# Moving the folding of W_v behind the placing of the scores in an attention and FFN kernel

## The reference, cut to what matters

```python
x: (64, 750, 1); W_tok: (512, 128); Wq, Wk, Wv, Wo: (512, 512); 16 heads of 32
patches = x[:, starts[:, None] + arange(128)]            # 10 positions, stride 64
h = patches @ W_tok.T + b                                # (64, 10, 512)
y = layernorm(h)
q, k, v = y @ Wq.T, y @ Wk.T, y @ Wv.T                   # by head; rope on q and k
scores = causal(q @ k.T / sqrt(32))
heavy = key with the largest sum of softmax(scores) over the queries
probs = softmax(scores where key is heavy or |i - j| <= 1)
h = h + (probs @ v) @ Wo.T
y = layernorm(h)
gate, up = split(y @ w_gate_up.T)                        # 2 x 2048
h = h + (silu(gate) * up) @ w_down.T
```

## Time and profile before

| | |
|---|---|
| median of 3 runs | 288.92 us (288.78 to 289.41) |
| the profiled execution | 288.86 us |
| its span, first to last instruction | 286.9 us |
| TensorE busy | 274.6 us, 96% |
| VectorE busy | 160.8 us, 56% |
| ScalarE busy | 80.3 us, 28% |
| POOL busy | 54.7 us, 19% |

### The profile page before, as it was taken

One profiled execution on the slowest core, in us unless ns is written; L12 is line 12 of the kernel. 1 busy time (PEld: TensorE's weight loads), 2 busy tenths in 40 slices (PEclk: granted clock), 3 DMA queues, 4 the chain that ended last, 5 costly groups with the idle time before them and its releaser, 6 DMA issues.

```text
span 286.9 us, 4588 instructions
## 1 busy us (share of the span) xinstructions
PE 274.6 (96%) x1781; PEld 215.9 (75%) x1781; DVE 160.8 (56%) x309; ACT 80.3 (28%) x151; POOL 54.7 (19%) x44
## 2 busy tenths in 40 slices
PE   7979999998899999999999999999999999999994
PEld 6455477664586877776876666799999999999993
DVE  2582987779669998696904435463333334333323
ACT  2211123431321001423011103263434444343320
POOL 0123000001006150003600000133222222332210
PEclk9999999999999999999999999999999999999999
DMA  7992130000002524353412033286334433330003
GB/s 226 425 404 82 43 112 0 5 2 0 1 2 110 163 102 177 116 193 130 144 77 73 37 112 111 110 271 243 110 111 146 148 142 110 110 110 0 0 0 110
DMA packets 6816, 32.76 MB, mean 114 GB/s; under 512 B 977, under 2 KB 977, under 8 KB 6289
## 3 DMA queue, kind: packets, MB, share of 16 engines
q1 hardware_dynamic: 6512, 32.15, 32.0%
q10 hardware_dynamic: 288, 0.39, 0.4%
HBM read 31.23 MB, written 1.31 MB: 113 GB/s over the span
## 4 chain that ended last, share of the span: by engine, by line
PE 91%; DVE 4%; ACT 1%; issue 1%; POOL 0%; DVEq 0%
PE ps L210 35%; PE ps L1076 20%; PE ps L1086 10%; PE ps L1013 6%; PE ps L951 4%; PE ps L1005 4%; PE ps L966 3%; PE ps L929 2%; PE ps L956 2%; PE ps L882 2%; PE ps L1018 1%; DVE prod L238 1%; PE ps L993 1%; PE ps L935 1%; DVE stats L553 1%
## 5 line engine op out<-in xcount | busy, mean ns | idle before, releaser
L210 PE MATMUL ps<-xT,wgu 128*128 128x384 f32 x384 | 70.9, 340 | 0.1
L210 PEld LDWEIGHTS ps<-xT,wgu 128*128 128x128 f32 x384 | 68.1, 188 | 2.5 <-DVE xT L584 0.9
L1076 PE MATMUL ps<-whole,stage 128*128 128x256 f32 (+1 forms) x288 | 58.3, 357 | 1.4 <-ACT whole L369 1.4
L1076 PEld LDWEIGHTS ps<-whole,stage 128*128 128x128 f32 x288 | 49.6, 190 | 12.2 <-issue 4.8
L789 DVE TENSOR_TENSOR gu<-silu,ps 128x256 f32<-128x256 f32 (+1 forms) x32 | 15.5, 484 | 67.6 <-PE ps L210 44.7
L303 POOL TENSOR_TENSOR wd<-stage,wd 128x512 fp32r<-128x512 f32 x16 | 26.9, 1681 | 78.6 <-ACT wd L369 78.6
L210 PE MATMUL ps<-wd,hT 128*128 128x512 f32 x144 | 35.6, 393 | 0.0
L474 ACT ACTIVATE silu<-ps 128x256 f32<-128x256 f32 (+1 forms) x32 | 14.0, 438 | 75.1 <-PE ps L1076 48.6
L210 PEld LDWEIGHTS ps<-wd,hT 128*128 128x128 f32 x144 | 26.8, 188 | 5.0
L1086 PE MATMUL ps<-stage,gu 128*128 128x512 f32 x64 | 30.1, 592 | 0.0
L369 ACT ACTIVATE wgu<-stage 128x1024 fp32r<-128x1024 f32 x16 | 16.9, 1058 | 22.7 <-PE ps L210 20.9
(11 more groups left out here) (101 smaller groups left out, 250.5 us busy)
## 6 DMA issues: line engine op xcount, KB each, us to landing
stage<-w_ffn SPq DMA_DIRECT2D x32, 768.0 KB, 4.3
stage<-w_k SPq DMA_DIRECT2D x1, 1024.0 KB, 6.7
stage<-w_q SPq DMA_DIRECT2D x1, 1024.0 KB, 10.1
stage<-w_v SPq DMA_DIRECT2D x1, 1024.0 KB, 12.2
wo<-w_o SPq DMA_DIRECT2D x1, 1024.0 KB, 13.9
out<-ob SPq DMA_DIRECT2D x14, 64.0 KB, 2.4
const<-consts SPq DMA_DIRECT2D x1, 800.0 KB, 8.1
out<-ob ACTq DMA_DIRECT2D x6, 64.0 KB, 1.9
```

Source lines behind the costliest of these rows:

```text
L210: ins = pe.matmul(dst, lhs[a], rhs[b], start=first and n == 0, stop=last and n == 2)
L1076: ins = pe.matmul(ps[:, bank, at + a:at + b], stage[:, slot, w:w + P], xf[:, k, a:b], start=k == 0, stop=k == KT - 1)
```

## The change

On TensorE `fold_weight(2)` goes from ahead of `score_sums(0)` to behind `score_place(1)`, straight ahead of the first projection of V. On ScalarE `folded(2)` and `folded_bias(2)` go from ahead of `chunk_out(0)` to behind exponentials 0 and 1, ahead of the drains. The other engines' lists are the same.

```diff
--- before.py
+++ after.py
@@ -447,12 +447,12 @@
             folded_bias(1)
             embedded(3)
             embedded(4)
-            folded(2)
-            folded_bias(2)
             chunk_out(0)
             chunk_out(1)
             for n in range(2):
                 exponential(n)
+            folded(2)
+            folded_bias(2)
             for item in DRAIN[:9]:
                 drain(item)
             for n in range(2, 4):
@@ -1038,12 +1038,12 @@
             project(("q", 0, 2), ("embedding", 2))
             embed(3, ("projection", ("k", 0, 0)))
             embed(4, ("projection", ("k", 0, 1)))
-            read_out("fold", 1)
-            fold_weight(2)
             score_sums(0, ("embedding", 3))
             score_place(0, ("embedding", 4))
             score_sums(1, ("projection", ("q", 0, 0)))
             score_place(1, ("projection", ("q", 0, 1)))
+            read_out("fold", 1)
+            fold_weight(2)
             project(("v", 0, 0), ("projection", ("k", 0, 2)))
             project(("v", 0, 1), ("chunk", 0))
             project(("v", 0, 2), ("projection", ("q", 0, 2)))
```

## The result

The changed kernel takes 294.53 us (median of 4 runs, 294.16 to 296.38), against 289.01 us before: a ratio of 1.020, with a 95% interval of 1.016 to 1.025. It is slower by 5.5 us. The forecast was 293.1 us in a range of 292.4 to 295.8. The direction and the wide range hold, and the point is 1.4 us too low. The forecast's own range, 292.6 to 293.5, was missed; the wide range holds because it was drawn out for the first rival, which had 0.22. That rival came true: the clock fell.

What follows compares the result with a forecast made beforehand. TensorE, 96% busy, bounds the kernel, with the projections setting when the value sums begin. Idle 3.64 plus 0.60 gives +4.24 us on 288.86, so 293.1 us (chance 0.72); own range 292.6 to 293.5, 8-in-10 range 292.4 to 295.8.

Steps and rivals of the forecast that it cites:

- the first rival: New idle stretch ahead of the score sums: clock falls from 2.4 to 1.2 GHz; 295.0 us, or 302.6 if lasting; chance 0.22.
- Step 1: First score sums: they wait for VectorE's product of query 6, start only 1.00 us earlier, leaving 3.64 us of new idle time.
- Step 2: Score sums and placings: the earlier start meets no new wait, their span stays 9.22 us, and the placing ends at 45.74.
- Step 3: Folding of W_v behind the second placing: ends at 50.38; ScalarE's moved exponentials are over some 2 us before and cost nothing.
- Step 4: Closing matmul of V's first projection: a new, uncovered wait for `fold_bias` through ScalarE and POOL, 0.60 us (0.52 to 0.70).
- Step 5: Load of `w_ffn[2]` into W_v's slot: issued at 50.4 instead of 37.5, costs nothing with over 30 us of cover.
- the rule: Trainium skill's warning that long TensorE idle gaps halve the clock, applied to the 3.64 us stretch: 295.0 us or more.
- The other side: End of the score path: scores, not projections, set the end, so the 1.00 us advance is the whole effect; 287.9 us, chance 0.03.
- The third rival: Value sums: their own 0.55 us wait takes up part of the delay, giving 292.5 us; chance 0.03.

Runs made afterwards that it cites:

- the late exponentials: The changed kernel with exponentials 0 and 1 moved back behind `folded_bias(2)` on ScalarE; 295.64 us (294.36 to 297.01).

## Why the prediction was right, and where its number was off

Step 1, the idle stretch ahead of the score sums: right. 3.75 us measured, 3.64 predicted. Filling it with matmuls nobody reads left the score sums where they were, so the product sets their start. The 0.11 us are the handover from VectorE: the product of query 6 ended at 33.93 + 1.96 = 35.89 by the chain, 0.14 us ahead of the matmul, and I had taken 0.04 (the difference that I took it from is itself 64.20 - 64.15 = 0.05).

Step 2, no new wait in the score sums: right. Their second half and both handovers took the same time as before. Only the first sums' length was off, which belongs to the clock.

Step 3, the moved exponentials cost nothing: right in this change (1.99 us of ScalarE's waiting between). The two variants where TensorE was earlier show the price without that cover: 2.15 us of idle time for the copies alone, and 0.93 instead of 0.55 us for the way of the bias when the bias part alone is moved.

Step 4, the bare way of the bias: right, 0.55 us by the chain, 0.60 predicted, and gone where the second score sums cover it. POOL's add took 0.48 us in its new place, near the undisturbed 0.46; my guess of a half disturbed one was on the high side.

Step 5, the load: right so far as the chain shows it; behind the value sums there is nothing but TensorE, and the shift of 5.27 us at 69 us is a shift of 5.3 us at the end.

What failed is the choice among the cases: the forecast put the clock at nothing, and it cost 1.71 us. The paragraph on the rule and the first rival had the mechanism, its place and its price: 1.9 us for a spell, against 1.71 measured, and 295.0 us as its time, against 294.53. The nearness is in part luck. The price came from the matmuls at the kernel's start, and the windows over these give a granted clock of 1.00 (1.45 to 5.02 us), so no row of the kernel before showed what half speed costs; and the last embedding happened to end 0.60 us earlier in the profiled execution, without which the same places give 5.90 us and not 5.30. I gave the rival 0.22 because the stretch of 1.75 us in the one profile had kept the clock. That row was one execution. Later ones show that the very same stretch loses the clock in two of five, so it never spoke for safety at twice the length. The four executions that the 289.01 us come from all lie at 289.41 or less, below every execution with a fallen clock. By the Trainium skill's "TensorE: Matmul & The Clock Gate", section "Why this matters for your kernels", a long idle gap between bursts of matmuls puts the clock back to half. The runs agree: the three profiles taken with the bare stretch of 3.75 us show the fall, and the mean clock of all 14 executions fits it. The heavier form of this rival, in which the score sums don't bring the clock back, did not happen: it was back during the first sums each time that a profile was taken.

The other side, that the score path sets the end, is refuted by the late exponentials. The third rival (part of it taken up by the value sums' wait) is refuted by the timeline of the changed kernel: that wait is 0.54 us where it was 0.55. The forecast's own range was added up 0.1 us short at its upper end (293.1 + 0.10 + 0.1 + 0.3 = 293.6), which changes nothing here.

## What to carry to other kernels

Work that stands between a producer on another engine and its consumer is cover, even if it looks like a delay of the consumer: before moving it, find when the consumer's input is really there, and count the difference as idle time. Count the clock with it: a new idle stretch on TensorE costs its own length, and it can cost a spell at half speed on whatever follows (here in all 14 executions at 3.75 us, in two of five at 1.75 us). And a short independent piece is best placed exactly in a handover, where TensorE waits for a copy anyway.

## What was not expected of the hardware

An idle stretch of 1.75 us on TensorE is a matter of luck: in 21 of 53 executions of the kernel before the mean clock was 0.994 or less, and with all but 0.21 us of the stretch filled it was so in none of the 26 executions of three kernels. It costs about 1.6 us each time (290.31 against 288.73 us, medians of one chip). Useless matmuls in such a gap shortened the median time of a kernel whose TensorE is the bound, from 289.24 to 288.77 us. What decides in a single execution whether the clock falls stays open. So does the one execution of the changed kernel at 296.38 us with a mean clock of 0.988, and the two with the late exponentials at 0.983; an early fall on top of the new one would fit the first, and so would one longer fall like that of 5.90 us above, but no profile of them was taken.
